# Two bias rows of a fused transformer block: VectorE sums bias times weights, TensorE multiplies once by ones

## The chip, the cores and the metric

One core of one Trainium2 chip runs the whole kernel. The metric is device time in microseconds (us) of one execution; the median of three runs stands for the kernel.

## The reference, cut to what matters

The block is two half-steps of a quantised feed-forward network around one attention, on x of 2 x 2048 rows of 256.

```python
x = x + 0.5 * ffn(layernorm(x))        # network 1
x = x + attn(layernorm(x))             # complex-valued projections, one softmax
x = x + 0.5 * ffn(layernorm(x))        # network 2

# inside attn; Wq, Wk, Wv are [512, 256], Wo is [256, 512], bq, bk, bv are [512]
scores = (qr @ kr.T + qi @ ki.T) / 16
out    = softmax(scores) @ [vr, vi] @ Wo.T + bo
```

ffn quantises its input, its weights and its hidden values in blocks of 16 to a four-bit grid. Attention is computed with products of the weights: M = Wq' Wk and N = Wv' Wo'. Two rows of 256 numbers come from the biases, the key row `bk @ Wq` (name `rk_row`) and the value row `bv @ Wo.T` (name `bias_row`, to which bo is added later). Each has to stand on all 128 partitions. This change is about how these two rows are made.

## The kernel before

The rows of x lie in SBUF as 32 tiles of 128 x 256. Every engine runs a program of its own in order; semaphores (`then_inc`, `wait_ge`) tie them together, and nothing reorders an engine's queue.

**Network 1** is a pipeline of rounds, `step(c, par)` with c from -2 to 29, and a tail for the last two tiles. A round works on several tiles at once. In round c TensorE runs, in this order: the first third of gate and up for tile c+3 (`gate_up`, L1881, its first matmul waits until VectorE has read the same PSUM banks for tile c+2), the transposes of the quantised values of tile c (L1762), the other two thirds of gate and up, and the down projection of tile c (L1892 with the upper halves, L1899 with the rest). Up to round 3 it also makes a product with a negative identity (L1920) for the lower halves; from c = 4 on VectorE makes these instead (`by_vector`, L894 and L896).

VectorE runs in round c: `scales(c + 2)` (L811 block maxima, L814, L824), `to_grid(c + 1)` (L833, L839), `lower(c)` (L894, L896) and `product(c + 3)` (L798, gate times up into `z`). The next thing is L811 of round c+1, which reads that `z` and a normalised tile from ScalarE.

GpSimd (POOL) runs in round c: `negative_scales` (L561, waits for L824), `residual` (L554), `scaled_by_pool(c + 2)` (L569, `y`; `product(c + 3)` waits for it, because it overwrites `z`) and `quantised(c + 1)` (L587, `zq`: three pieces of 256, 704 and 64 columns). If c divides by four it also runs `group_std` (L482 to L490), and if c - 1 does, `output_std` (L497 to L503). L798, L833, L839 and L894 have one operand in PSUM and one in SBUF; L569 and L587 read two tensors in SBUF.

**The bias rows.** Wq lies in SBUF as `wq_s` [128, 4, 256] and Wo transposed as `woT` [128, 4, 256]: 512 rows in four groups of 128. `b3` holds the three biases as [128, 3, 4]. During the start GpSimd spreads bk and bv over 128 columns each (`broadcast_biases`, `bkB` and `bvB`, L540 and L541). Late in network 1, in round 29, TensorE makes the key row (`key_bias_row`): four matmuls of plain float32, one per group, summed in PSUM, with the spread bias as stationary operand, so that every partition receives the row. At the beginning of attention, between the transposes of the second group of keys and the first values, it makes the value row the same way (`value_bias_row`). All of these show as L1769, the line of the helper `product`, and a float32 matmul stands in the trace as two records. ScalarE copies both rows out (`bias_rows`, L1313 and L1314), which frees the bank, and VectorE and GpSimd use them.

At the beginning of attention VectorE runs the lower halves of the keys (L975), `row_term` per tile (L777, needs `rk_row`) and the lower halves of the values (L989); `values(0, 2)` on TensorE waits for the first L989.

Of the kernel before, what the change touches and what calls it, by code (L numbers as in the profile page):

```python
# [9 lines left out]
ALU = mybir.AluOpType  # L10
# [3 lines left out]
P = 128  # L14
# [16 lines left out]
def macaron_kernel(nc, x_in, wq, bq, wk, bk, wv, bv, wo, bo, w_gate, w_up, w_down, out):  # L31
    T, D = x_in.shape
# [7 lines left out]
    KE = E // P  # L40
# [26 lines left out]
    with ctx:  # L67
        def sb(name, shape, dt=F32, at=ctx):
            return at.enter_context(nc.sbuf_tensor(name, shape, dt))
# [4 lines left out]
        def sem(name):  # L74
            return ctx.enter_context(nc.semaphore(name))
# [10 lines left out]
        m_hi = sb("m_hi", [P, KD, D], F32R)  # L86
        m_lo = sb("m_lo", [P, KD, D], F32R)
        nv = sb("nv", [P, KD, 2 * D], F32R)
# [19 lines left out]
        ffn = ExitStack()  # L108
# [14 lines left out]
        wq_s = sb("wq_s", [P, KE, D], at=ffn)  # L123
        woT = sb("woT", [P, KE, D], at=ffn)
        b3 = sb("b3", [P, 3, KE], at=ffn)
        bkB = sb("bkB", [P, KE, P], at=ffn)
        bvB = sb("bvB", [P, KE, P], at=ffn)
        bo_row = sb("bo_row", [P, D], at=ffn)
        mv = sb("mv", [P, NT, 2], at=ffn)
        stats = sb("stats", [P, NT, 6], at=ffn)  # L130
# [55 lines left out]
        rk_sum, bv_sum = bank4[:, 2, 0:D], bank4[:, 2, D:2 * D]  # L186
# [8 lines left out]
        qk_in, wv_in, wo_in, b_in = sem("qk_in"), sem("wv_in"), sem("wo_in"), sem("b_in")  # L195
# [1 line left out]
        x_in_s = [sem(f"x_in{n}") for n in range(len(x_parts))]  # L197
        wc = {k: sem("w_" + k) for k in ("amax", "up", "neg", "inv", "y", "y_pool", "abs", "rnd", "grid", "q", "T", "hi",
                                         "sub", "lo")}
        aw = {k: sem("aw_" + k) for k in ("bcast", "bk", "row", "row_s", "woT", "woT_s", "m", "m_hi", "m_sub", "m_lo", "nv", "nv_hi",  # L200
                                          "nv_sub", "nv_lo", "bq", "bq_s", "rows", "rows_s", "bias")}
        x_tot, x_nm, x_var, x_eps = sem("x_tot"), sem("x_nm"), sem("x_var"), sem("x_eps")
        stat_set, mv_done, g_stats, g_rstd, g_nmr = (sem("stat_set"), sem("mv_done"), sem("g_stats"),
# [41 lines left out]
        def hidden(k):  # L245

            return between(k, 0, NT - 1)

        def ahead(k):

            return between(k, -LEAD, NT - LEAD - 1)
# [5 lines left out]
        def number(f, k):  # L257

            return NCH * f + k + LEAD + 1
# [10 lines left out]
        def whole(f, k):  # L270

            return (3 if f else 2) <= k <= NT - LEAD - 1
# [6 lines left out]
        def wait_scaled(engine, f, k):  # L279

            if hidden(k) and not whole(f, k):
                engine.wait_ge(y_done, scaled_apart(f, k))
            if ahead(k):
                engine.wait_ge(yx_done, NT * f + k + LEAD + 1)
# [27 lines left out]
        def T_bank(k):  # L312

            return bank5[:, 0:2, :] if k == NT - 2 else bank2[:]
# [139 lines left out]
        def _(pool):  # L454
# [80 lines left out]
                pool.wait_ge(aw["m"], 1)  # L535
                nc.gpsimd.tensor_copy(wk_s[:, :, D], b3[:, 1, :]).then_inc(aw["bk"], 1)

            def broadcast_biases():

                nc.gpsimd.tensor_copy(bkB[:], b3[:, 1, :].unsqueeze(2).to_broadcast([P, KE, P]))  # L540
                nc.gpsimd.tensor_copy(bvB[:],  # L541
                                      b3[:, 2, :].unsqueeze(2).to_broadcast([P, KE, P])).then_inc(aw["bcast"], 1)

            def output_bias():

# [72 lines left out]
            weight_q(3)  # L618
            bias_column()
            first_ffn(-5, 1)  # L620
            broadcast_biases()
            first_ffn(-4, 0)
            pool.wait_ge(wc["y"], 2)
            weight_y(5)
# [88 lines left out]
        def _(dve):  # L713
# [6 lines left out]
            def group_statistics(g):  # L720

                tiles = range(4 * g, 4 * g + 4)
                q = slice(tiles[0], tiles[-1] + 1)
                dve.wait_ge(stat_set, tiles[-1] - 7)
                for t in tiles:
                    nc.vector.bn_aggr(mv[:, t, :], stats[:, t, :]).then_inc(mv_done, 1)
                dve.wait_ge(mv_done, tiles[-1] - 7)
                nc.vector.tensor_scalar(out=nmean[:, q], in0=mv[:, q, 0], scalar1=-1.0, scalar2=None,
                                        op0=ALU.mult).then_inc(g_stats, 1)
                nc.vector.tensor_scalar(out=var[:, q], in0=mv[:, q, 1], scalar1=EPS, scalar2=None,  # L730
                                        op0=ALU.add).then_inc(g_stats, 1)
# [59 lines left out]
            def ffn_step(f):  # L791
                def product(t):

                    dve.wait_ge(silu_done, NT * f + t + 1)
                    dve.wait_ge(gu_done, NT * f + t + 1)
                    if t and whole(f, t - 1):
                        wait_scaled(dve, f, t - 1)
                    nc.vector.tensor_tensor(out=z[:, 0:I], in0=gu[:, I:G], in1=silu[:],  # L798
                                            op=ALU.mult).then_inc(gu_read, 1)
# [57 lines left out]
                def blocks_of(c, par):  # L857
                    if c == NT - 3:
                        scales(NT - 1, par)
                        scaled(NT - 1)  # L860
                        to_grid(NT - 2)
                        quantised_late(NT - 2, 1 - par)
                        return
                    if c < -3 and chain(c + 1):
                        to_grid(c + 1)
                    if chain(c + 2):
                        scales(c + 2, par)
                    if f == 0 and c == -2:
                        scaled(c + 2)
                        to_grid(c + 1)  # L870
                        return
                    if c >= -3 and chain(c + 1):
                        to_grid(c + 1)
                    if chain(c + 2) and not whole(f, c + 2):
                        scaled(c + 2)
                    if by_vector(f, c):
                        lower(c, par)

                def input_statistics(c):

                    if c == -2:
                        tile_statistics(8)
                        tile_statistics(9)
                    if c == -1:
                        tile_statistics(10)
                        tile_statistics(11)
                        group_statistics(2)

                def lower(k, par):

                    bank = T_bank(k).rearrange("p a (n t) -> p (a n) t", t=P)
                    dve.wait_ge(hi_done, number(f, k))
                    n = slice(0, HK + KD if ahead(k) else HK)
                    nc.vector.tensor_tensor(out=T_lo[:, par, n, :], in0=bank[:, n, :],  # L894
                                            in1=T_hi[:, par, n, :].bitcast(F32), op=ALU.subtract)
                    nc.vector.tensor_tensor(out=T_hi[HR:P, par, HK + KD, :], in0=bank[HR:P, HK + KD, :],  # L896
                                            in1=T_hi[HR:P, par, HK + KD, :].bitcast(F32),
                                            op=ALU.subtract).then_inc(vector_lo, 1)
# [15 lines left out]
                def quantised_late(k, par):  # L914

                    dve.wait_ge(grid_done, number(f, k))
                    dve.wait_ge(T_done, number(f, k - 1))
                    nc.vector.tensor_tensor(out=blocks(zq[:, 0:I]), in0=blocks(grid[:, 0:I]),
                                            in1=spread(s_neg[:, par, 0:HB], HB), op=ALU.mult)
                    nc.vector.tensor_tensor(out=blocks(zq[:, I:I + HR]), in0=blocks(grid[:, I - HR:I]),  # L920
                                            in1=spread(s_neg[:, par, HB - HR // BLOCK:HB], HR // BLOCK),
                                            op=ALU.mult).then_inc(zq_done, 1)
# [7 lines left out]
                def step(c, par):  # L930
                    blocks_of(c, par)
                    if hidden(c + 3):
                        product(c + 3)
                    if f == 0 and c < 0:
                        input_statistics(c)
                    if c == NT - 2:
                        quantised_late(NT - 1, 1 - par)
                        lower_late(c, par)
                    if c == NT - 1:
                        lower_late(c, par)  # L940
                        if f:
                            residual_last()
# [231 lines left out]
            n = NQ - 1  # L1174
# [581 lines left out]
        def _(pe):  # L1756
# [10 lines left out]
            def product(dst, left, right, first=True):  # L1767
                for j in range(KE):
                    last = nc.tensor.matmul(dst, lhsT=left[:, j, :], rhs=right[:, j, :],  # L1769
                                            start=first and j == 0, stop=j == KE - 1, skip_group_check=True)  # L1770
                return last
# [60 lines left out]

            def key_bias_row():

                pe.wait_ge(aw["bcast"], 1)
                product(rk_sum, bkB, wq_s).then_inc(aw["rows"], 1)

            def value_bias_row():

                product(bv_sum, bvB, woT, False).then_inc(aw["rows"], 1)  # L1840

            def weight_lower(n):

# [415 lines left out]
            n = NQ - 1  # L2259
# [67 lines left out]
```

## Time and profile before

| | |
|---|---|
| median of 3 runs | 908.06 us (907.93 to 908.46) |
| the profiled execution | 908.92 us |
| its span | 907.1 us |
| granted TensorE clock, mean | 1.000 of full speed |
| network 1 in the rows | from about 20 us to 258 us |
| TensorE busy | 884.5 us (98%) |
| VectorE busy | 693.5 us (76%) |
| GpSimd busy | 548.2 us (60%) |

The span is that of the recorded instructions. A busy share is an average over stages: in network 1, network 2 and attention the engines are loaded differently. Matmul records overlap their neighbours, so the time that a matmul takes from its engine is the distance between starts.

### The profile page before, as it was taken

The page shows a single profiled execution, that of the slowest core. Times are in us where ns is not written, and L with a number is a line of the kernel's source. Part 1 is how long each engine was busy: PE and PEld are TensorE (multiplying, and loading weights), DVE is VectorE, ACT ScalarE, POOL GpSimd, SP SyncE. Part 2 cuts the span into 40 slices and gives each one's busy share as a digit, 9 for nine tenths or more (in the row PEclk, how much of TensorE's full clock was granted, in tenths as well). Part 3 has the DMA queues.
Part 4 walks back from the last instruction along what each step waited for, and adds up shares of the span by engine and source line. Part 5 has one row for each costly group of instructions (what it writes and reads, how often), then busy time and mean ns, then how long its engine had stood idle before and what let it go on. Part 6 is the DMA issues. An engine that isn't in the chain of part 4 may idle for free.

```text
span 907.1 us, 16197 instructions
## 1 busy us (share of the span) xinstructions
PE 884.5 (98%) x5608; PEld 796.5 (88%) x5608; DVE 693.5 (76%) x1088; ACT 620.5 (68%) x1383; POOL 548.2 (60%) x618
## 2 busy tenths in 40 slices
PE   4999999999999999999999999999999999999997
PEld 3789999999987898999998899998998899999997
DVE  6987999999976667654564644545599999999998
ACT  6789888877674665768675576767784567555453
POOL 5477889898410264535763154546477778877762
DMA  9200000000000000000000000000000000000001
GB/s 314 66 1 1 1 1 2 1 1 1 1 1 1 1 1 1 1 1 2 1 1 1 1 1 1 1 1 1 1 1 1 1 24 24 25 24 24 1 24 47
DMA packets 11952, 13.81 MB, mean 15 GB/s; under 512 B 864, under 2 KB 11104, under 8 KB 11872
## 3 DMA queue, kind: packets, MB, share of 16 engines
q1 hardware_dynamic: 11872, 12.79, 4.2%
q8 instruction: 45, 0.74, 0.3%
q14 instruction: 35, 0.29, 0.1%
HBM read 8.59 MB, written 4.19 MB: 14 GB/s over the span
## 4 chain that ended last, share of the span: by engine, by line
PE 88%; DVE 5%; ACT 2%; issue 2%; POOL 2%; DMA 1%; SPq 0%; DVEq 0%; POOLq 0%; ACTq 0%
PE bank L1881 24%; PE bank L2135 19%; PE bank_b L1892 7%; PE bank L1762 7%; PE bank_b L1899 5%; PE bank L2175 4%; PE bank L2177 4%; PE bank L2173 4%; PE bank L2098 2%; PE bank_b L2177 1%; PE bank_b L2173 1%; PE bank_b L2175 1%; PE bank L2116 1%; PE bank_b L2116 1%; DMA wk_s<-in_L_attn_Wk 1%
## 5 line engine op out<-in xcount | busy, mean ns | idle before, releaser
L637 POOL TENSOR_TENSOR p_lo<-s_ring,p_hi 128x512 fp32r<-128x512 f32 x128 | 167.3, 1311 | 217.6 <-ACT p_hi L1620 217.6
L1004 DVE TENSOR_TENSOR top<-bank,top 128x512 f32<-128x512 f32 x112 | 77.4, 691 | 125.7 <-ACT s_ring L1604 125.6
L587 POOL TENSOR_TENSOR zq<-grid,s_neg 128x256 f32<-128x256 f32 (+2 forms) x184 | 141.9, 798 | 14.3 <-DVE grid L839 14.3
L1881 PE MATMUL bank<-w_hi,T_hi 128*128 128x512 f32 (+1 forms) x384 | 148.8, 387 | 1.3 <-DVE z L798 0.9
L1881 PE MATMUL bank<-w_hi,T_lo 128*128 128x512 f32 (+1 forms) x384 | 144.0, 375 | 0.0
L1881 PE MATMUL bank<-w_lo,T_hi 128*128 128x512 f32 (+1 forms) x384 | 143.6, 374 | 0.0
L1604 ACT ACTIVATE s_ring<-bank 128x512 f32<-128x512 f32 x128 | 75.9, 593 | 78.0 <-PE bank L2135 77.9
L1425 ACT ACTIVATE T_hi<-bank 128x1024 fp32r<-128x1024 f32 (+1 forms) x68 | 64.7, 951 | 84.9 <-PE bank L1762 84.9
L2173 PE MATMUL bank<-v_hl,p_hi 128*128 128x258 f32 x384 | 110.0, 286 | 0.4 <-DVE x L1036 0.2
L2175 PE MATMUL bank<-v_hl,p_hi 128*128 128x256 f32 x384 | 108.3, 282 | 0.0
L2177 PE MATMUL bank<-v_hl,p_lo 128*128 128x258 f32 x384 | 108.3, 282 | 0.0
L569 POOL TENSOR_TENSOR y<-z,s_inv 128x960 f32<-128x960 f32 (+1 forms) x56 | 98.5, 1758 | 8.9 <-DVE s_inv L824 4.5
L2135 PE MATMUL bank<-q_hi,k_hi 128*128 128x512 f32 x256 | 101.3, 396 | 0.8
L2135 PE MATMUL bank<-q_lo,k_hi 128*128 128x512 f32 x256 | 100.7, 393 | 0.0
L2135 PE MATMUL bank<-q_hi,k_lo 128*128 128x512 f32 x256 | 100.3, 392 | 0.0
L1610 ACT ACTIVATE s_ring<-s_ring 128x512 f32<-128x512 f32 x128 | 79.2, 622 | 18.5 <-DVE s_ring L1026 18.5
L1026 DVE TENSOR_TENSOR s_ring<-s_ring,bank 128x512 f32<-128x512 f32 x128 | 84.9, 678 | 1.3 <-PE bank L1762 0.9
L1620 ACT ACTIVATE p_hi<-s_ring 128x512 fp32r<-128x512 f32 x128 | 80.7, 631 | 7.1 <-PE bank_b L2177 3.5
L811 DVE TENSOR_REDUCE amax<-z 128x60 f32<-128x960 f32 (+2 forms) x72 | 74.9, 1041 | 11.8 <-ACT z L1459 9.0
L1881 PEld LDWEIGHTS bank<-w_hi,T_hi 128*128 128x128 f32 x384 | 72.3, 188 | 11.3 <-issue 1.2
L1881 PEld LDWEIGHTS bank<-w_hi,T_lo 128*128 128x128 f32 x384 | 72.2, 188 | 10.6
L1892 PE MATMUL bank_b<-wd_hl,T_hi 128*128 128x256 f32 x600 | 80.4, 280 | 0.1
(239 smaller groups left out, 2232.0 us busy)
## 6 DMA issues: line engine op xcount, KB each, us to landing
out<-x SPq DMA_DIRECT2D x7, 512.0 KB, 2.9
x<-in_L_attn_hidden_states SPq DMA_DIRECT2D x3, 1024.0 KB, 12.2
x<-in_L_attn_hidden_states SPq DMA_DIRECT2D x2, 512.0 KB, 7.7
wraw<-in_L_ffn_w_down SPq DMA_DIRECT2D x1, 704.0 KB, 7.5
wraw<-in_L_ffn_w_up SPq DMA_DIRECT2D x1, 640.0 KB, 5.5
wq_s<-in_L_attn_Wq SPq DMA_DIRECT2D x1, 512.0 KB, 7.1
wk_s<-in_L_attn_Wk SPq DMA_DIRECT2D x1, 512.0 KB, 8.0
wo_s<-in_L_attn_Wo SPq DMA_DIRECT2D x1, 512.0 KB, 8.3
```

The source lines that it names most:

```text
L569: nc.gpsimd.tensor_tensor(out=blocks(y[:, lo:Z]), in0=blocks(z[:, lo:Z]), in1=spread(s_inv[:, lo // BLOCK:ZB], (Z - lo) // BLOCK), op=ALU. ...
L587: last = nc.gpsimd.tensor_tensor(out=blocks(zq[:, to:to + hi - lo]), in0=blocks(grid[:, lo:hi]), in1=spread(s_neg[:, par, lo // BLOCK:hi / ...
L637: nc.gpsimd.tensor_tensor(out=lower_buf(n, c), in0=score_buf(n, c), in1=upper_buf(n, c).bitcast(F32), op=ALU.subtract).then_inc(plo_done, 1)
L1026: nc.vector.tensor_tensor(out=p, in0=p, in1=shift_bank, op=ALU.subtract).then_inc(diff_done, 1)
L1610: nc.scalar.activation(p, p, ACT.Exp, scale=SCALE).then_inc(exp_done, 1)
L1620: nc.scalar.activation(upper_buf(n, c), score_buf(n, c), ACT.Copy).then_inc(phi_done, 1)
L1881: last = nc.tensor.matmul(gu[:, lo:hi], lhsT=T[:, par, HK + kd, :], rhs=w[:, kd, lo:hi], start=n == 0, stop=n == len(terms) - 1)
L1892: nc.tensor.matmul(dn, lhsT=T_hi[:, par, k, :], rhs=wd_hl[:, k, half:half + D], start=n == 0, stop=False)
L2135: last = nc.tensor.matmul(score_bank(c), lhsT=kk[:, kd, t], rhs=q[:, kd, :], start=i == 0, stop=i == len(terms) - 1)
L2173: nc.tensor.matmul(o[:, 0:D + 2], lhsT=hi[:, q], rhs=v_hl[:, c, 0:D + 2], start=c == 0, stop=False, skip_group_check=True)
L2175: nc.tensor.matmul(o[:, 0:D], lhsT=hi[:, q], rhs=v_hl[:, c, D + 2:], start=False, stop=False, skip_group_check=True)
L2177: last = nc.tensor.matmul(o[:, 0:D + 2], lhsT=lo[:, q], rhs=v_hl[:, c, 0:D + 2], start=False, stop=c == CH - 1, skip_group_check=True)
```

## The change

VectorE now sums bias times weights over the four groups ahead of time, in eight instructions: for each row one `tensor_scalar` and three `scalar_tensor_tensor` over 128 x 256 float32, all operands in SBUF. They stand in VectorE's queue behind `product(c + 3)` of rounds 4, 6, 8, ..., 18 of network 1. What is left is a sum over partitions, which TensorE makes with one float32 matmul per row and a square of ones as stationary operand. GpSimd writes that square with one memset, where it spread the biases with two copies. SBUF space of the two spread biases goes to `bias_sum` and `ones_sq`. `product(dst, left, right)` is the loop of four matmuls.

```diff
-            def broadcast_biases():
-                nc.gpsimd.tensor_copy(bkB[:], b3[:, 1, :].unsqueeze(2).to_broadcast([P, KE, P]))
-                nc.gpsimd.tensor_copy(bvB[:],
-                                      b3[:, 2, :].unsqueeze(2).to_broadcast([P, KE, P])).then_inc(aw["bcast"], 1)
+            def all_ones():
+                nc.gpsimd.memset(ones_sq[:], 1.0).then_inc(aw["ones"], 1)
...
             first_ffn(-5, 1)
-            broadcast_biases()
+            all_ones()
             first_ffn(-4, 0)
...
+                def bias_part(i):
+                    n, j = i // KE, i % KE
+                    weights = (wq_s, woT)[n]
+                    if i == 0:
+                        dve.wait_ge(b_in, 16 * 4)
+                        dve.wait_ge(qk_in, 16 * 2)
+                    if i == KE:
+                        dve.wait_ge(aw["woT_s"], 2)
+                    if j == 0:
+                        nc.vector.tensor_scalar(out=bias_sum[:, n, :], in0=weights[:, 0, :], scalar1=b3[:, 1 + n, 0:1],
+                                                scalar2=None, op0=ALU.mult).then_inc(aw["sum"], 1)
+                    else:
+                        dve.wait_ge(aw["sum"], i)
+                        nc.vector.scalar_tensor_tensor(out=bias_sum[:, n, :], in0=weights[:, j, :],
+                                                       scalar=b3[:, 1 + n, j:j + 1], in1=bias_sum[:, n, :],
+                                                       op0=ALU.mult, op1=ALU.add).then_inc(aw["sum"], 1)
...
                     if hidden(c + 3):
                         product(c + 3)
+                    if f == 0 and 4 <= c < 4 + 4 * KE and c % 2 == 0:
+                        bias_part(c // 2 - 2)
...
             def key_bias_row():
-                pe.wait_ge(aw["bcast"], 1)
-                product(rk_sum, bkB, wq_s).then_inc(aw["rows"], 1)
+                pe.wait_ge(aw["ones"], 1)
+                pe.wait_ge(aw["sum"], KE)
+                nc.tensor.matmul(rk_sum, lhsT=ones_sq[:], rhs=bias_sum[:, 0, :], start=True, stop=True,
+                                 skip_group_check=True).then_inc(aw["rows"], 1)
             def value_bias_row():
-                product(bv_sum, bvB, woT, False).then_inc(aw["rows"], 1)
+                pe.wait_ge(aw["sum"], 2 * KE)
+                nc.tensor.matmul(bv_sum, lhsT=ones_sq[:], rhs=bias_sum[:, 1, :], start=False, stop=True,
+                                 skip_group_check=True).then_inc(aw["rows"], 1)
```

## Rows read from the trace of the kernel before

**Rows 1.** The page: VectorE's busy tenths in 40 slices of the span.

```profile
DVE  6987999999976667654564644545599999999998
```

**Rows 2.** Window of four rounds: us, busy PE, PEld, DVE, ACT, POOL, clock.

```profile
137.30:164.02 26.72, 26.72 (x175) 24.50 (x174) 25.10 (x33) 23.31 (x72) 23.28 (x31) 1.00 0.01 1
```

**Rows 3.** VectorE's timeline in network 1: start, us, line, [idle before].

```profile
84.45 0.89 DVE L798 TENSOR_TENSOR z<-bank,silu 128x704 f32<-128x704 f32 x1
85.43 1.15 DVE L811 TENSOR_REDUCE amax<-z 128x60 f32<-128x960 f32 x1
...
97.83 0.89 DVE L798 TENSOR_TENSOR z<-bank,silu 128x704 f32<-128x704 f32 x1 [0.18 <-POOL y L569]
...
104.32 0.89 DVE L798 TENSOR_TENSOR z<-bank,silu 128x704 f32<-128x704 f32 x1
...
184.06 0.89 DVE L798 TENSOR_TENSOR z<-bank,silu 128x704 f32<-128x704 f32 x1
185.21 1.15 DVE L811 TENSOR_REDUCE amax<-z 128x60 f32<-128x960 f32 x1 [0.25 <-ACT z L1459]
```

**Rows 4.** TensorE's timeline: first matmul of a round.

```profile
85.49 0.47 PE L1881 MATMUL bank<-w_hi,T_hi 128*128 128x512 f32 x1
...
185.79 0.40 PE L1881 MATMUL bank<-w_hi,T_hi 128*128 128x512 f32 x1
```

**Rows 5.** GpSimd's timeline; x2 are the 256 and the 704 piece.

```profile
83.98 1.97 POOL L587 TENSOR_TENSOR zq<-grid,s_neg 128x256 f32<-128x256 f32 x2
...
97.66 1.97 POOL L587 TENSOR_TENSOR zq<-grid,s_neg 128x256 f32<-128x256 f32 x2
```

**Rows 6.** Durations (ns, min/median/max) of VectorE instructions of 128 x 256, all in SBUF.

```profile
L777 DVE SCALAR_TENSOR_TENSOR st_junk<-x,nmean,rk_row x32: 474/480/1612, 264.5 to 395.1; 128x256 f32<-128x256 f32 x32
L1075 DVE TENSOR_SCALAR xn<-x,nmean,rstd x6: 397/404/1414, 454.1 to 459.1; 128x256 f32<-128x256 f32 x6
```

**Rows 7.** Timeline: VectorE and GpSimd at the same time.

```profile
309.48 1.60 DVE L777 SCALAR_TENSOR_TENSOR st_junk<-x,nmean,rk_row 128x256 f32<-128x256 f32 x1
309.51 1.29 POOL L637 TENSOR_TENSOR p_lo<-s_ring,p_hi 128x512 fp32r<-128x512 f32 x1 [0.37 <-ACT p_hi L1620]
...
458.74 1.74 DVE L1075 TENSOR_SCALAR xn<-x,nmean,rstd 128x256 f32<-128x256 f32 x2
459.03 1.30 POOL L637 TENSOR_TENSOR p_lo<-s_ring,p_hi 128x512 fp32r<-128x512 f32 x1 [1.38 <-ACT p_hi L1620]
```

**Rows 8.** TensorE's timeline at the two bias rows and at `values(0, 2)`.

```profile
246.35 1.89 PE L1769 MATMUL bank<-wq_s,bkB 128*128 128x256 f32 x8
247.89 0.82 PE L1920 MATMUL bank<-T_hi,neg_ident 128*128 128x512 f32 x2
...
261.78 1.89 PE L1769 MATMUL bank<-woT,bvB 128*128 128x256 f32 x8
263.32 0.59 PE L2116 MATMUL bank<-nv,k_hi 128*128 128x256 f32 x2
...
267.11 0.48 PE L2116 MATMUL bank<-nv,k_hi 128*128 128x256 f32 x2
```

**Rows 9.** Timelines of ScalarE and VectorE beside the bias rows.

```profile
246.57 1.01 ACT L1425 ACTIVATE T_hi<-bank 128x1024 fp32r<-128x1024 f32 x1
...
253.53 0.22 DVE L920 TENSOR_TENSOR zq<-grid,s_neg 128x64 f32<-128x64 f32 x1
...
263.03 1.23 DVE L975 TENSOR_TENSOR k_lo<-bank,k_hi 128x1024 fp32r<-128x1024 f32 x1 [0.46 <-ACT k_hi L1369]
...
265.92 0.69 DVE L989 TENSOR_TENSOR v_hl<-bank,v_hl 128x512 fp32r<-128x512 f32 x1
```

**Rows 10.** Timeline of the start: VectorE and GpSimd.

```profile
24.30 0.61 POOL L540 COPY bkB<-b 128x512 f32<-128x512 f32 x1
24.32 0.63 DVE L819 SCALAR_TENSOR_TENSOR s_neg<-amax,c_neg 128x16 f32<-128x16 f32 x1
...
48.17 0.89 DVE L798 TENSOR_TENSOR z<-bank,silu 128x704 f32<-128x704 f32 x1
```

More of the change, by code:

```diff
@@ L125, in macaron_kernel @@
         b3 = sb("b3", [P, 3, KE], at=ffn)
-        bkB = sb("bkB", [P, KE, P], at=ffn)
-        bvB = sb("bvB", [P, KE, P], at=ffn)
+        bias_sum = sb("bias_sum", [P, 2, D], at=ffn)
+        ones_sq = sb("ones_sq", [P, P], at=ffn)
         bo_row = sb("bo_row", [P, D], at=ffn)
@@ L199, in macaron_kernel @@
                                          "sub", "lo")}
-        aw = {k: sem("aw_" + k) for k in ("bcast", "bk", "row", "row_s", "woT", "woT_s", "m", "m_hi", "m_sub", "m_lo", "nv", "nv_hi",
+        aw = {k: sem("aw_" + k) for k in ("ones", "sum", "bk", "row", "row_s", "woT", "woT_s", "m", "m_hi", "m_sub", "m_lo", "nv", "nv_hi",
                                           "nv_sub", "nv_lo", "bq", "bq_s", "rows", "rows_s", "bias")}
```

## The prediction, made before the changed kernel was run

> **What bounds the kernel now.** I read the page first, its totals (in the table above) and then its slices: TensorE is busy nearly always, VectorE three quarters of the span, but VectorE's slices stand at 9 through most of network 1, where its eight new instructions go [rows 1]. So the question is whether VectorE has room there. Then comes a window of four rounds: from 137.30 on they take 26.72 us, TensorE is busy in all of it, VectorE for 25.10 [rows 2]. VectorE's own timeline shows the room more sharply. The shortest distance between two L798 is 6.49 us (97.83 to 104.32), against 26.72 / 4 = 6.68 for TensorE, and in a settled round VectorE waits 0.25 us for ScalarE ahead of L811 [rows 3]. That is 0.19 to 0.25 us of room per round.
>
> How late VectorE may be is seen from L798's end to TensorE's first matmul of the next round. In the first round that matters it is 85.49 - (84.45 + 0.89) = 0.15 us, which is as tight as it gets: TensorE waits there. Late in the stage it is 185.79 - (184.06 + 0.89) = 0.84 [rows 3, 4]. So VectorE starts with no reserve at round 4 and has saved up 0.84 - 0.15 = 0.69 us by round 19.
>
> **The change part by part.** *The eight VectorE instructions.* The nearest rows for their size: a `scalar_tensor_tensor` of 128 x 256 with all operands in SBUF takes 0.48 us in the median but 1.61 at most, a `tensor_scalar` 0.40 and 1.41 [rows 6]. The long ones are explained by GpSimd. At 309.48 the vector instruction meets a GpSimd one that ends at 309.51 + 1.29 = 310.80; it ends at 311.08, 0.28 later. At 458.74 the second of two `tensor_scalar` meets one that ends at 460.33 and ends itself at 460.48, 0.15 later [rows 7]. So such an instruction runs only when GpSimd's instruction is through, and then takes 0.28 or 0.15 us. The Trainium skill says the same ("SBUF — State Buffer", section "SBUF: two separate sides"): the port pair that the two engines share is an exclusive lock for a whole instruction, and it bears on vector instructions with two SBUF inputs or in a two-port mode. By that rule the sum is the one worked out next; it speaks against this change, since VectorE's big instructions in these rounds each have an operand in PSUM and the new ones don't.
>
> What does GpSimd do when the new instruction comes up, directly behind L798? In round 4 its 256 and 704 pieces of `zq` begin at 83.98 and end at 85.95, which is 1.50 us behind L798's start at 84.45. In round 6 they end at 99.63, 1.80 behind the start at 97.83 [rows 3, 5]. L798 is through 0.9 us behind its start. So all eight come up inside the 704 piece. This isn't chance: the distance hangs on GpSimd's chain behind L824 of the same round, so it moves with VectorE when VectorE gets late. The next L811 then starts about 1.75 us behind L798's start (0.65 + 0.98 with `tensor_scalar`) in place of 0.98 (84.45 to 85.43): 0.75 us, or 0.65. In the rounds like 6, where GpSimd is late from its two extra groups (L798 waits 0.18 for it there [rows 3]), it is 2.05 - 0.98, about 1.05.
>
> Now VectorE over four rounds. From L798 of round 4 to that of round 6: 2 x 6.49 + 0.65 = 13.63. GpSimd alone gives 97.83 - 84.45 = 13.38, and 0.25 for being held by the new instruction in its turn, also 13.63. From round 6 to 8: 2 x 6.49 + 1.05 = 14.03. Sum 27.66, against TensorE's 26.72: 0.94 too much. Three such groups bring L798 of round 16 to 84.45 + 83.0 = 167.4, and that of round 19 comes 13.63 + 1.05 + 6.49 = 21.2 later, at 188.6. Before it stood at 184.06 [rows 3]. VectorE is 4.5 us late, less the reserve of 0.69: TensorE stalls 3.8 us, spread over rounds 5 to 19, a part in nearly every second one. After the last of them VectorE's room hides the rest, and the stall stays in the span, since TensorE has no idle time to take it from.
>
> *The key row.* Its four matmuls take 247.89 - 246.35 = 1.54 us [rows 8]; three of four are 1.16. But they stand ahead of L1920, which waits for ScalarE's `T_hi`, and that ends at 246.57 + 1.01 = 247.58 [rows 9]. So L1920 can come at 247.7 at best, 0.2 us earlier. Behind it VectorE works without a pause on the last two tiles and ends its `zq` at 253.75 [rows 9], which the last transposes wait for; it gains next to nothing from this. I take 0.1 us (bounds 0 and 0.25).
>
> *The value row.* Again 263.32 - 261.78 = 1.54, so 1.16 less [rows 8]. Values follow at once and need nothing from it. What is late next is the first lower half of values on VectorE, which stands behind L975 (263.03 to 264.26 [rows 9], unmoved, since it waits for ScalarE's keys) and two `row_term` of some 0.5 us [rows 6], and takes 0.69 itself [rows 9]: it ends at about 264.26 + 1.1 + 0.7 = 266.1. The values that wait for it start at 267.11 now and would want to come at 267.11 - 1.16 = 265.95 [rows 8]. So I take 1.0 us (bounds 0.8 and 1.16).
>
> *GpSimd's start.* Two copies go, the first of 0.61 us [rows 10], and one memset comes. Meanwhile VectorE's L819 of 16 columns takes 0.63 us, most of it held by the copy [rows 10]. About 0.5 us come free on VectorE. But its queue is fed again by the first L798, which waits for TensorE, and TensorE's round waits for the third L798 (48.17 [rows 10]), up to which VectorE has no pause. I take 0.05 us (bounds 0 and 0.35, the idle time of ScalarE and TensorE on that way). The added waits cost nothing: GpSimd used the same biases at 24.30 [rows 10], 60 us before the first of the eight, and the last one comes up near 182, over 60 us before TensorE asks for the key row at 246.35 [rows 8].
>
> Sum: + 3.8 - 0.1 - 1.0 - 0.05 = + 2.65 us. The profiled execution took 908.92 us for a span of 907.1, 0.9 above the median of 908.06; against the median the forecast is **910.7 us**. Some 1.8 us (0.2%) is what a measurement of this kernel can tell from no change.
>
> **The rivals.**
> *A, the forecast:* held, 910.7, own range 909.5 to 911.8. A milder form has the two engines share the way instead of locking it: each costs some 0.4 + 0.27, a pair 1.34, four rounds 25.96 + 1.34 = 27.3, which over 15 rounds and with 0.3 for the first is a stall of 2.5 and 909.4. 65% in all.
> *B, not slower:* the eight aren't held. Place: VectorE between L798 and L811; price 0.4 us each (0.48 less the overlap), 25.96 + 0.8 = 26.76 in four rounds, just TensorE's pace. The stall is 0.4 (0.2 of it at round 5, where there is no reserve), 1.15 come off: 907.3. It decides as soon as an instruction costs under some 0.5 us, where the stall falls under 1.15. For it: the median rows are short. Against it: the phase of the 704 piece. 18%.
> *C, faster:* as B, and both bias rows give their whole 1.16: 2.3 less 0.3, 906.0. Against it: `T_hi` ends 0.3 us ahead of L1920 [rows 8, 9]. 5%.
> *D, worse:* the new instruction gets its turn only behind the 64 piece too, and GpSimd's `zq` gets late for the transposes: 0.3 us more in each of eight, 913.1. For it: the three pieces follow each other without a gap. Against it: nothing in the rows shows a vector instruction passed over. 12%.
>
> **How the numbers follow.** The time is A's. The range reaches down to B with its scatter and up to D: 906.9 to 913.1; C and the tails are left out. Slower by over 0.2%: A without its milder part, 55%, and D, 12%: 67%. Within: the rest of A, 10%, and B: 28%. Faster: C, 5%.
>
> **What would show it.** The eight instructions of 128 x 256 should take 0.6 to 1.2 us in the trace and end 0.15 or 0.28 us behind a 704 piece; if they take 0.4 to 0.5, B holds. Four rounds between L798 of rounds 4 and 20 should take 27.6 us, not 26.7, with TensorE idle ahead of L1881 and released by L798. L1920 of round 29 should come right behind `T_hi`, with TensorE idle for about 1 us ahead of it. The first values' lower half should set `values(0, 2)`. The prediction is wrong if GpSimd's pieces move away from L798 once VectorE is late, or if VectorE catches up between two new instructions by more than 0.2 us per round.

## The result, and the profile after

The changed kernel takes 910.84 us (median of 8 runs, 910.55 to 911.29), the kernel before 908.09 (median of 8, 907.76 to 908.55). The ratio is 1.003, its 95% interval 1.002 to 1.0039: slower by some 2.7 us, against a forecast of 910.7. The profiled execution has a span of 909.5 us (before 907.1) at a granted clock of 1.00 of full speed (mean).

The totals and VectorE's slices on the page of the changed kernel:

```profile
PE 885.0 (97%) x5596; PEld 793.9 (87%) x5596; DVE 697.8 (77%) x1096; ACT 621.4 (68%) x1383; POOL 549.1 (60%) x617
DVE  7987999999986766665573644545599999999998
```

VectorE's slices hardly differ from [rows 1] (the last one of network 1 is at 8 for 7): tenths are too coarse for this change. The line numbers have moved: L796 is the L798 of the rows before, L809 the L811, L585 the L587, L1903 the L1881, L1921 the L1899 and L1942 the L1920. The windows view, four rounds at a time, from one L796 to the fourth behind it (columns as in rows 2):

```profile
84.06:111.67 27.61, 27.37 (x171) 24.48 (x171) 26.79 (x35) 22.39 (x67) 23.52 (x31) 1.00 0.00 1
111.67:139.41 27.74, 27.48 (x174) 24.74 (x173) 26.91 (x34) 22.68 (x69) 23.65 (x31) 1.00 0.00 1
139.41:167.03 27.62, 27.35 (x174) 24.70 (x173) 26.78 (x34) 23.46 (x71) 23.53 (x31) 1.00 0.01 2
```

Four rounds take 27.6 to 27.7 us (forecast 27.66), where they took 26.72 at TensorE's own pace [rows 2]. (The first two groups of four, from round 4 and from round 8, took 26.37 and 26.48 between two L798 before, because VectorE was catching up there.) VectorE is busy for 26.8 of them, 1.7 more than the 25.1 before, and what is left is 0.8 us, the few hundredths between its instructions. TensorE, which had no idle time there, has some in every one. The group that costs it, from the view of one tile (ns: min/median/max, then first and last start):

```profile
L901 DVE SCALAR_TENSOR_TENSOR bias_sum<-wq_s,b,bias_sum x3: 973/1272/1277, 98.5 to 126.2; 128x256 f32<-128x256 f32 x3
L901 DVE SCALAR_TENSOR_TENSOR bias_sum<-woT,b,bias_sum x3: 973/1273/1276, 153.9 to 181.6; 128x256 f32<-128x256 f32 x3
...
L897 DVE TENSOR_SCALAR bias_sum<-wq_s,b x1: 847/847/847, 84.9 to 84.9; 128x256 f32<-128x256 f32 x1
L897 DVE TENSOR_SCALAR bias_sum<-woT,b x1: 846/846/846, 140.2 to 140.2; 128x256 f32<-128x256 f32 x1
```

Why they take that long is seen in the timeline of round 6, first VectorE, then GpSimd:

```profile
97.68 0.89 DVE L796 TENSOR_TENSOR z<-bank,silu 128x704 f32<-128x704 f32 x1
98.48 1.28 DVE L901 SCALAR_TENSOR_TENSOR bias_sum<-wq_s,b,bias_sum 128x256 f32<-128x256 f32 x1
99.69 1.14 DVE L809 TENSOR_REDUCE amax<-z 128x60 f32<-128x960 f32 x1
...
105.18 0.89 DVE L796 TENSOR_TENSOR z<-bank,silu 128x704 f32<-128x704 f32 x1
```

```profile
95.72 1.82 POOL L567 TENSOR_TENSOR y<-z,s_inv 128x960 f32<-128x960 f32 x1
97.51 2.40 POOL L585 TENSOR_TENSOR zq<-grid,s_neg 128x256 f32<-128x256 f32 x3
101.73 0.41 POOL L559 TENSOR_SCALAR s_neg<-amax 128x60 f32<-128x60 f32 x1 [1.81 <-DVE s_inv L822]
```

The 256 and 704 pieces of `zq` take 1.97 us together [rows 5], so the second ends at 97.51 + 1.97 = 99.48. The new instruction starts at 98.48 and ends at 99.76, 0.28 behind that. Then L809 starts at 99.69, 2.01 behind L796, where it stood 0.98 behind it before [rows 3]. GpSimd's third piece, 64 columns, pays too: the three take 2.40 us here and 2.23 in the round before, which has no new instruction. The last row shows what GpSimd does with the delay: it waits 1.81 us for VectorE's scales. Both engines are late, and GpSimd has no more work than before. Of VectorE's 1.28 us only 0.48 are work: that is what the same kind of instruction takes alone [rows 6].

The waits view for 85 to 200 us (in total, times, longest):

```profile
POOL s_neg L559 <- DVE s_inv L822: 13.5, 12, 1.8
PEld bank_b L1921 <- DVE T_hi L912: 2.0, 5, 0.5
...
PE bank_b L1921 <- DVE T_hi L912: 1.0, 4, 0.3
```

And TensorE's timeline at one of the waits:

```profile
105.20 0.50 PE L1921 MATMUL bank_b<-wd_hl,T_hi 128*128 128x256 f32 x2 [0.24 <-DVE T_hi L912]
105.55 0.75 PE L1921 MATMUL bank_b<-wd_hl,T_lo 128*128 128x256 f32 x5
106.22 0.47 PE L1903 MATMUL bank<-w_hi,T_hi 128*128 128x512 f32 x1
```

L1903 starts 0.15 us behind the end of L796 (105.18 + 0.89 = 106.07), the distance at which TensorE waited in the first tight round before. The idle time that the profile names, though, stands one step earlier, ahead of L1921, which wants the last lower part of `T` that VectorE makes just ahead of L796.

The two bias rows on TensorE, and the values that are late next:

```profile
249.96 0.60 PE L1855 MATMUL bank<-bias_sum,ones_sq 128*128 128x256 f32 x2
251.25 0.73 PE L1942 MATMUL bank<-T_hi,neg_ident 128*128 128x512 f32 x2 [0.69 <-ACT T_hi L1443]
...
265.12 0.60 PE L1861 MATMUL bank<-bias_sum,ones_sq 128*128 128x256 f32 x2
265.36 0.58 PE L2138 MATMUL bank<-nv,k_hi 128*128 128x256 f32 x2
```

The account, in the differences of start against the same instruction before: at L796 of round 4 the kernel is 0.39 us early (84.06 for 84.45), at that of round 19 it is 4.22 late (188.28 for 184.06). The reserve takes up part of that, and at L796 of round 28, the last tile, it is 3.61 late (247.57 for 243.96): TensorE has lost 4.0 us. The first matmul of the queries is 3.34 late, so the key row gave 0.27. The first matmul of the scores is 2.28 late, so the value row gave 1.06. From there to the end of the span it is 638.5 us before and 638.6 after.

### The profile page after: what moved, and what is told of

Read it like the earlier page. It is cut to its first block, busy times and chain, and to the rows that moved or that the text cites. A ratio compares the mean times of both kernels' runs of the same rounds, so it can differ in the third digit from the quotient of the medians.

```text
span 909.5 us, 16181 instructions
## 1 busy us (share of the span) xinstructions
PE 885.0 (97%) x5596; PEld 793.9 (87%) x5596; DVE 697.8 (77%) x1096; ACT 621.4 (68%) x1383; POOL 549.1 (60%) x617
## 4 chain that ended last, share of the span: by engine, by line
PE 72%; DVE 4%; POOL 3%; issue 1%; ACT 1%; DVEq 0%; POOLq 0%
PE bank L2157 19%; PE bank L1903 16%; PE bank_b L1914 5%; PE bank L1780 5%; PE bank L2199 4%; PE bank L2197 4%; PE bank L2195 4%; PE bank_b L1921 4%; PE bank L2120 2%; POOL p_lo L635 2%; PE bank_b L2199 1%; PE bank_b L2195 1%; PE bank_b L2197 1%; PE bank L2138 1%; PE bank_b L2138 1%
## 5 line engine op out<-in xcount | busy, mean ns | idle before, releaser
L585 POOL TENSOR_TENSOR zq<-grid,s_neg 128x256 f32<-128x256 f32 (+2 forms) x184 | 143.1, 805 | 13.8 <-DVE grid L837 13.8
L1903 PE MATMUL bank<-w_hi,T_hi 128*128 128x512 f32 (+1 forms) x384 | 149.3, 389 | 1.2 <-DVE z L796 1.1
L1903 PE MATMUL bank<-w_hi,T_lo 128*128 128x512 f32 (+1 forms) x384 | 143.8, 374 | 0.0
L1903 PE MATMUL bank<-w_lo,T_hi 128*128 128x512 f32 (+1 forms) x384 | 143.4, 374 | 0.0
L1903 PEld LDWEIGHTS bank<-w_hi,T_hi 128*128 128x128 f32 x384 | 72.2, 188 | 11.8 <-issue 1.2
L809 DVE TENSOR_REDUCE amax<-z 128x60 f32<-128x960 f32 (+2 forms) x72 | 74.8, 1038 | 9.0 <-ACT z L1477 6.1
L1903 PEld LDWEIGHTS bank<-w_hi,T_lo 128*128 128x128 f32 x384 | 72.1, 188 | 10.8
```

Of the source, the lines that this page charges most:

```text
L585: last = nc.gpsimd.tensor_tensor(out=blocks(zq[:, to:to + hi - lo]), in0=blocks(grid[:, lo:hi]), in1=spread(s_neg[:, par, lo // BLOCK:hi / ...
L1903: last = nc.tensor.matmul(gu[:, lo:hi], lhsT=T[:, par, HK + kd, :], rhs=w[:, kd, lo:hi], start=n == 0, stop=n == len(terms) - 1)
```

## The experiments

Experiments 1 to 4 are compared with the kernel before at a median of 908.37 us, experiments 5 to 7 with it at 907.99, each measured alongside. Differences of a few tenths between the two sets are not read. Each diff is against the changed kernel, and waits that belong to a changed line change with it where they are not shown. The question is how much of the 2.7 us is VectorE's held instructions, whether the hold is GpSimd's lock or simply the place of more work, and whether TensorE's gain is real by itself.

**1. VectorE's part alone.**

```
-                nc.gpsimd.memset(ones_sq[:], 1.0).then_inc(aw["ones"], 1)
+                nc.gpsimd.tensor_copy(bkB[:], b3[:, 1, :].unsqueeze(2).to_broadcast([P, KE, P]))
+                nc.gpsimd.tensor_copy(bvB[:],
+                                      b3[:, 2, :].unsqueeze(2).to_broadcast([P, KE, P])).then_inc(aw["bcast"], 1)
...
-                nc.tensor.matmul(rk_sum, lhsT=ones_sq[:], rhs=bias_sum[:, 0, :], start=True, stop=True,
-                                 skip_group_check=True).then_inc(aw["rows"], 1)
+                product(rk_sum, bkB, wq_s).then_inc(aw["rows"], 1)
...
-                nc.tensor.matmul(bv_sum, lhsT=ones_sq[:], rhs=bias_sum[:, 1, :], start=False, stop=True,
-                                 skip_group_check=True).then_inc(aw["rows"], 1)
+                product(bv_sum, bvB, woT, False).then_inc(aw["rows"], 1)
```

> VectorE's eight instructions stay in rounds 4 to 18, their sums are not used; the bias rows are made as before (two copies on GpSimd, four matmuls each). If the stall in network 1 is VectorE's alone, its L798 distances are those of the changed kernel (four rounds 27.6 to 27.7 us) and nothing is given back: about 908.1 + 3.9 = 912.0 us. If part of the stall came from TensorE's or GpSimd's new queue, it is clearly under that, 911 or less.

Measured: 912.23 us (911.62 to 912.46, 5 runs), ratio 1.0042 (1.0028 to 1.0055). The start of L796 goes from 0.84 early in round 4 to 3.23 late in the last one: 4.07 us. The eight instructions are the same ones, 0.84 to 0.85 and 0.98 to 1.28 us. So VectorE's part costs about 4 us by itself, and the new matmuls on TensorE have no share in it.

**2. TensorE's part alone.**

```
+                nc.gpsimd.memset(bias_sum[:], 0.0)
                 nc.gpsimd.memset(ones_sq[:], 1.0).then_inc(aw["ones"], 1)
...
-                    if f == 0 and 4 <= c < 4 + 4 * KE and c % 2 == 0:
-                        bias_part(c // 2 - 2)
```

> The eight VectorE instructions are left out (GpSimd writes zeros into the sums during the start, so the two bias rows are zero); one matmul per row. Theory of the prediction: 0.1 + 1.0 + 0.05 come off, 906.9 us. What the trace of the changed kernel shows (0.4 at the start, 0.25 at the key row, 1.05 at the value row) gives 906.4. Rival: the removed matmuls come off whole, 2.6 us, 905.5.

Measured: 906.68 us (906.35 to 906.95, 11 runs), ratio 0.9981 (0.9972 to 0.999). Every distance between two L796 of network 1 is that of before to some hundredths. The gain stands in the two places: 0.27 us behind the key row and 1.06 behind the value row, 1.3 in the trace for 1.7 (plus or minus 0.8) in the medians. The whole 1.16 for each is out.

**3. The same eight instructions in other slots of the round.** Behind the block maximum, where GpSimd has finished `zq` and waits for the scales, in two neighbouring rounds of each four.

```
+            BIAS_AT = (7, 8, 11, 12, 15, 16, 19, 20)
...
                                             apply_absolute_value=True).then_inc(amax_done, 1)
+                    if f == 0 and k - 2 in BIAS_AT:
+                        bias_part(BIAS_AT.index(k - 2))
...
-                    if f == 0 and 4 <= c < 4 + 4 * KE and c % 2 == 0:
-                        bias_part(c // 2 - 2)
```

> The same eight instructions, with the same operands, but between L809 and L812 of rounds 7, 8, 11, 12, 15, 16, 19, 20, where GpSimd stands idle and waits for VectorE's scales. Theory of the hold: none of them meets a GpSimd instruction, each takes 0.40 to 0.48 us, four rounds take 26.7 to 26.9, and what the matmuls and the start give stays: 906.5 to 907.3 us. Rival, VectorE has no room for this work wherever it stands (0.75 to 1.05 us are what such an instruction costs in these rounds): 910.8 as the changed kernel.

Measured: 908.58 us (908.28 to 909.15, 11 runs), ratio 1.0003 (0.9995 to 1.0012). The instructions ran as expected, but the kernel is 1.3 us slower than the expectation allows. Two rows of its VectorE timeline, at different times:

```profile
99.47 0.35 DVE L811 TENSOR_SCALAR bias_sum<-wq_s,b 128x256 f32<-128x256 f32 x1
...
233.42 0.74 DVE L839 SCALAR_TENSOR_TENSOR s_neg<-amax,c_neg 128x44 f32<-128x44 f32 x1
```

The first is a bias instruction, not held: 0.35 us for the 0.85 of the changed kernel, and the `scalar_tensor_tensor` take 0.48 for 0.97 to 1.28. So the place makes the price, and over half of it is waiting. The second is far behind the last bias instruction and explains part of the miss. It is an old instruction of 44 columns, and GpSimd's row at that time is

```profile
233.31 0.79 POOL L552 TENSOR_TENSOR x<-x,down 128x256 f32<-128x256 f32 x1 [1.25 <-ACT down L1434]
```

The rounds themselves lost 0.77 us (L796's counterpart from 0.44 early to 0.33 late): four rounds take 26.8 to 26.9, just over TensorE's 26.72, and VectorE arrives in the last rounds with less reserve: in round 25 its product ends 0.61 us ahead of TensorE's next first matmul, for 0.84 before. In the rounds that follow, a small VectorE instruction and GpSimd's residual come up almost together, and the one that starts first decides. In the kernel before `s_neg` starts 0.12 us ahead of the residual in round 26 and takes 0.20; here it starts 0.11 behind and takes 0.74. In experiment 1 it is ahead by just 0.02, and is not held; its rows, first VectorE, then GpSimd:

```profile
236.41 0.20 DVE L820 SCALAR_TENSOR_TENSOR s_neg<-amax,c_neg 128x44 f32<-128x44 f32 x1
```

```profile
236.43 0.78 POOL L555 TENSOR_TENSOR x<-x,down 128x256 f32<-128x256 f32 x1 [1.37 <-ACT down L1435]
```

In experiment 3 one small instruction in each of rounds 26, 27 and 28 is held: 0.74, 0.57 and 0.65 us in place of 0.20. The first queries are 1.28 late, 0.95 more than at round 26, although the key row gives back 0.27 ahead of them: 1.2 us for the tail. 0.8 + 1.2 = 2.0, and the run is 1.9 above experiment 2.

**4. The same place, a quarter of the columns.**

```
-                        nc.vector.tensor_scalar(out=bias_sum[:, n, :], in0=weights[:, 0, :], scalar1=b3[:, 1 + n, 0:1],
+                        nc.vector.tensor_scalar(out=bias_sum[:, n, 0:D // 4], in0=weights[:, 0, 0:D // 4], scalar1=b3[:, 1 + n, 0:1],
...
-                        nc.vector.scalar_tensor_tensor(out=bias_sum[:, n, :], in0=weights[:, j, :],
+                        nc.vector.scalar_tensor_tensor(out=bias_sum[:, n, 0:D // 4], in0=weights[:, j, 0:D // 4],
```

> The eight instructions at their place, on 64 of 256 columns (the other three quarters of both sums are left out and zero). Theory of the hold: only the streaming gets shorter (0.2 us of scalar_tensor_tensor, 0.1 of tensor_scalar); they still end right behind the 704 piece and last 0.65 to 1.1 us; four rounds 27.2 to 27.3, 909.2 to 909.6 us. Rival, the cost is the work itself or a shared rate, in proportion to the width: 0.2 us each, hidden, 906.5 to 907 us.

Measured: 909.54 us (909.11 to 910.86, 11 runs), ratio 1.0016 (1.0007 to 1.0024). A quarter of the work still costs two thirds: four rounds take 27.3 us. VectorE and GpSimd in round 6:

```profile
98.11 1.07 DVE L902 SCALAR_TENSOR_TENSOR bias_sum<-wq_s,b,bias_sum 128x64 f32<-128x64 f32 x1
```

```profile
97.13 2.23 POOL L586 TENSOR_TENSOR zq<-grid,s_neg 128x256 f32<-128x256 f32 x3
```

The 704 piece ends at 97.13 + 1.97 = 99.10, the instruction at 99.18, 0.08 behind it where the full one is 0.28 behind. All eight are 0.75 to 1.08 us, 0.1 to 0.2 shorter than the full ones, and three quarters of the columns are gone. That rules out the milder form of A, in which two engines share the way and a shorter instruction is shorter in proportion. From round 4 to round 25 the rounds lose 2.73 us (the changed kernel has lost 4.06 there). The profiled execution then has the held small instructions of experiment 3 as well (0.75, 0.57 and 0.64 us) and is the slowest of the eleven, 910.86; 1.3 us less for that tail is 909.5, the median. That most of the others were spared the tail is inferred from this sum, not seen.

**5. All eight instructions in VectorE's pause behind network 1.** Both rows are then made just ahead of the values.

```
             first_residual_last()
+            for i in range(2 * KE):
+                bias_part(i)
...
                         pe.wait_ge(gu_read, NT)
-                        key_bias_row()
...
             transpose_keys(0, 1)
+            key_bias_row()
             value_bias_row()
```

(The call of `bias_part` in the rounds goes, as in experiment 3.)

> All eight instructions in one row behind VectorE's last residual of network 1, where VectorE waits 2.3 us for ScalarE's queries and GpSimd is idle; both bias rows are made next to each other at the place of the value row. Theory of the hold: 0.35 to 0.42 us each, 2.9 in all, of which 0.6 stand out of the pause and delay only the lower halves of the queries, which TensorE needs 6 us later; network 1 is that of the kernel without them. 906.7 to 907.0 us, as the kernel with one matmul and no vector work (906.7). Rival: VectorE's work is paid for there too, since keys, values and row terms follow: 908 and more.

Measured: 906.77 us (906.63 to 907.58, 11 runs), ratio 0.9987 (0.9979 to 0.9996). VectorE's timeline of the pause:

```profile
257.38 0.41 DVE L943 SCALAR_TENSOR_TENSOR x<-bank,x 128x256 f32<-128x256 f32 x1
257.71 0.34 DVE L799 TENSOR_SCALAR bias_sum<-wq_s,b 128x256 f32<-128x256 f32 x1
258.09 1.52 DVE L803 SCALAR_TENSOR_TENSOR bias_sum<-wq_s,b,bias_sum 128x256 f32<-128x256 f32 x3
259.53 0.35 DVE L799 TENSOR_SCALAR bias_sum<-woT,b 128x256 f32<-128x256 f32 x1
259.91 1.52 DVE L803 SCALAR_TENSOR_TENSOR bias_sum<-woT,b,bias_sum 128x256 f32<-128x256 f32 x3
261.36 1.40 DVE L997 SCALAR_TENSOR_TENSOR q_lo<-bank,bqk,q_hi 128x512 fp32r<-128x512 f32 x2
```

and GpSimd's, which says why nothing holds them:

```profile
256.49 0.74 POOL L552 TENSOR_TENSOR x<-x,down 128x256 f32<-128x256 f32 x1 [2.40 <-ACT down L1432]
263.25 0.74 POOL L545 TENSOR_TENSOR bias_row<-bias_row,bo_row 128x256 f32<-128x256 f32 x1 [6.03 <-ACT bias_row L1332]
```

Eight instructions that cost 4 us in the rounds take 3.7 us of VectorE's time here and cost nothing that is seen. The 3.7 are more than the 2.9 expected, since a `scalar_tensor_tensor` takes 0.48 us here too. L997 follows at once, 1.0 us later than before if the 0.2 by which this trace is early are taken off, and no wait of TensorE comes of it: from the first values to the first scores it is 5.28 us, as before. At the scores this trace has gained 1.14 us where experiment 2 has 1.33; the 0.2 belong to the key row's matmul, which stands ahead of the values now. The median is under that of the kernel before by 1.2 us (0.1%, interval 0.04 to 0.21%), and under that of the changed kernel by about 4.

**6. A mixture:** the key's four in the slots of experiment 3 (rounds 7, 8, 11 and 12), the value's four in the pause.

```
+            BIAS_AT = (7, 8, 11, 12)
...
             first_residual_last()
+            for i in range(KE, 2 * KE):
+                bias_part(i)
```

> The four instructions of the key row between L809 and L812 of rounds 7, 8, 11, 12, the four of the value row in the pause behind the last residual. Theory: the kernel with all eight in such slots lost some 0.7 us in rounds 26 to 28, where a late VectorE ran into GpSimd's residual (L552) with small instructions; with only four, VectorE has caught up before that, so four rounds take 26.7 to 26.8 and the last L796 distances are 6.98, 6.45, 6.39 as before: 906.8 to 907.3 us. Rival: the losses at the end have nothing to do with how late VectorE is: 907.5 to 908.

Measured: 906.95 us (906.64 to 907.65, 11 runs), ratio 0.9986 (0.9977 to 0.9995). The run is there for experiment 3's miss: VectorE has time to catch up behind round 12. The start of `z` (L816 here) goes from 0.76 early in round 4 to 0.15 late in round 14 and back to 0.46 early in round 20, and stays there, 0.3 us lost in all. In the last rounds the small instruction now passes ahead of GpSimd's residual, first VectorE, then GpSimd:

```profile
232.63 0.20 DVE L839 SCALAR_TENSOR_TENSOR s_neg<-amax,c_neg 128x44 f32<-128x44 f32 x1
```

```profile
232.75 0.74 POOL L552 TENSOR_TENSOR x<-x,down 128x256 f32<-128x256 f32 x1 [1.47 <-ACT down L1436]
```

The distances of the last three rounds are 6.97, 6.45 and 6.39 us, those of before, against 6.98, 6.98 and 6.55 in experiment 3. VectorE's product of round 26 ends 0.54 us ahead of TensorE's next first matmul, as before, against 0.31 in experiment 3. So the 1.2 us of that tail hang on some 0.2 us of VectorE's reserve, as the trace of experiment 3 suggested.

**7. Experiment 2 with GpSimd's two copies kept.**

```
+                nc.gpsimd.tensor_copy(bkB[:], b3[:, 1, :].unsqueeze(2).to_broadcast([P, KE, P]))
+                nc.gpsimd.tensor_copy(bvB[:], b3[:, 2, :].unsqueeze(2).to_broadcast([P, KE, P]))
+                nc.gpsimd.memset(bias_sum[:], 0.0)
                 nc.gpsimd.memset(ones_sq[:], 1.0).then_inc(aw["ones"], 1)
```

> As the kernel with one matmul per row and no vector work (sums left out, both rows zero), but GpSimd still makes the two copies during the start, ahead of its memsets. Theory of the prediction: what the copies cost VectorE is covered, at most 0.1 us more than without them, 906.7 to 906.8. Rival, taken from the start of the changed kernel's trace, which is 0.4 us ahead: 907.0 to 907.1.

Measured: 906.77 us (906.37 to 907.93, 11 runs), ratio 0.9988 (0.9979 to 0.9997), against 0.9981 (0.9972 to 0.999) without the copies. The intervals overlap: the copies are worth some tenths at most. The traces say the same. The second `z` starts 0.3 to 0.9 us earlier than in the trace of before in all eight new traces, and the two that keep the copies are 0.84 and 0.93 early.

## Why the prediction was right, step by step

**The hold.** It was the main term, and it held in form and size. All eight instructions start 0.80 to 0.81 us behind L796, inside the 704 piece, and end 0.28 to 0.29 (`scalar_tensor_tensor`) or 0.16 (`tensor_scalar`) behind its end. Experiments 3, 4 and 5 show the mechanism from three sides: away from GpSimd's pieces the same instruction takes 0.48 us and not 1.27; with a quarter of the columns in the old place it still takes 1.07; in the pause the eight are free. That the place directly behind L796 is slow for another reason doesn't fit either: in rounds 8 and 16 the `scalar_tensor_tensor` comes up 1.28 us behind the start of `zq` and takes 0.97 us, in rounds 6, 10, 14 and 18 it comes up 0.97 to 0.99 behind and takes 1.27 to 1.28. No run moved GpSimd's pieces themselves. The rule cited in the prediction from the Trainium skill ("SBUF — State Buffer", section "SBUF: two separate sides") agrees with all of that. The same section says that a GpSimd instruction that only writes SBUF doesn't contend with a VectorE instruction of two SBUF inputs, and one pair of rows agrees: in experiment 4, GpSimd's memset of 512 columns at 23.88 (0.52 us) and VectorE's two-input instruction of 16 columns at 23.89 (0.16 us) ran side by side:

```profile
23.89 0.16 DVE L818 SCALAR_TENSOR_TENSOR s_neg<-amax,c_neg 128x16 f32<-128x16 f32 x1
```

```profile
23.88 0.52 POOL L540 MEMSET bias_sum<- 128x512 f32 x1
```

Before, the same instruction took 0.63 us beside GpSimd's copy, which reads SBUF [rows 10].

**VectorE's lateness.** Forecast 27.66 per four rounds, measured 27.61, 27.74 and 27.62; forecast 4.5 by round 19, measured 0.39 + 4.22 = 4.6. **TensorE's stall:** forecast 3.8, measured 4.0, and 4.07 in experiment 1. The term was too small by 0.2: VectorE was late by 4.6 and not 4.5, and from round 19 to 28 it won back 0.6 and not 0.69. Where it shows was told only in part: L1903 does start 0.15 behind L796's end, but the named idle time stands ahead of L1921, released by the end of `T`'s lower part on VectorE. Also, the profile shows TensorE idle for only 0.24 to 0.27 us in windows that are 0.9 to 1.0 longer than the 26.72 of TensorE's own pace. The rest stands in records that got longer, such as first matmuls of 0.50 us where 0.40 is usual, and in the waits of weight loads, so distances between the same instruction are the safer measure of a stall.

**The key row.** Forecast 0.1, bound 0.25, measured 0.27 to 0.28, just outside the bound, in the changed kernel and in experiments 2, 6 and 7. It is 0.27 in experiment 5 too, where no key row stands in that place at all, so it isn't the matmuls that limit it. The limit was told rightly: L1942 waits 0.69 for ScalarE's `T_hi` at 251.20. What was mis-sized is what lies behind: the last tile's work on ScalarE and VectorE moved up with it (the L831 of the last `zq` is 3.40 late where L796 is 3.61), and I had taken VectorE as the bound there, working "without a pause". It does wait there: before, that last L833 starts at 250.87, when ScalarE's `silu` has ended at 250.78. The idle time forecast as about 1 us is 0.69.

**The value row.** The saving ahead of the values was forecast as 1.16, three quarters of 1.54. Measured is 1.30: the first values start 0.24 behind the one matmul (265.12 to 265.36), so a row of four had 1.54 and one has 0.24. Then 0.24 is given back: L1007 ends at 268.55 + 0.69 = 269.24 and `values(0, 2)` starts at 269.39, 2.28 late, the first lower half of values being what sets it, as forecast. Net 1.06, forecast 1.0.

The size of this term is right, but the prediction reached it by a step that it didn't check. It gave VectorE 1.1 us for the two `row_term` ahead of that lower half, from the median of [rows 6]. In the kernel before they took 1.66 us at this very place (264.26 to 265.92), because the first one waited for ScalarE's copy of the value row and was then held by GpSimd's addition of bo, which starts on the same copy. First VectorE, then GpSimd, before:

```profile
264.47 0.99 DVE L777 SCALAR_TENSOR_TENSOR st_junk<-x,nmean,rk_row 128x256 f32<-128x256 f32 x1 [0.21 <-ACT bias_row L1314]
```

```profile
264.44 0.74 POOL L547 TENSOR_TENSOR bias_row<-bias_row,bo_row 128x256 f32<-128x256 f32 x1 [6.73 <-ACT bias_row L1314]
```

and in the changed kernel:

```profile
267.52 0.58 DVE L775 SCALAR_TENSOR_TENSOR st_junk<-x,nmean,rk_row 128x256 f32<-128x256 f32 x1
```

```profile
267.08 0.73 POOL L545 TENSOR_TENSOR bias_row<-bias_row,bo_row 128x256 f32<-128x256 f32 x1 [6.03 <-ACT bias_row L1332]
```

The shorter value row brings copy and addition forward, the wait is gone and all but a tenth of the hold, and the two take 0.96 us (267.59 to 268.55). Experiments 2 and 7 show the same (0.59 and 0.58 for the first one), and experiment 1, with four matmuls, has the 0.99 back. Had the 1.66 stayed, `values(0, 2)` would have started 0.7 us later, and the value row would have given some 0.4 (an estimate from these rows). That the forecast of 1.0 came true rests on an effect that it doesn't name, and to that extent it is luck.

**The start.** Forecast 0.05. The first L796 waited 0.60 us for TensorE, so what VectorE gained ahead of it ends there, as said. All eight new traces are early at the second `z`, the two that keep the copies too (experiments 1 and 7), so this isn't the edit's doing. It fits the trace of before instead, whose execution took 908.92 us, 0.9 above the median; the changed kernel's took 911.29, 0.45 above its own. The difference, 0.4, is about the 0.39 by which the trace is early at round 4. The other traces fit, experiment 4 with its tail apart: the later the second `z`, the longer the profiled execution against the median of its own kernel (0.93 early and at the median in experiment 2, 0.29 early and 0.8 above it in experiment 5). So executions of one kernel differ ahead of the second `z`. What varies there was not looked for.

**The sum:** +4.0 - 0.27 - 1.06 = +2.7 at the scores without the start, and the medians differ by 2.7; with the start it is +2.3, and the spans differ by 2.4. The forecast time is within 0.2 us of the measured one, closer than its terms deserve: the stall was 0.2 larger than forecast, and the two savings together 0.2 larger, which cancels. Experiments 1 and 2, which are the two halves, give +3.9 and -1.7 in the medians, together +2.2, which differs from 2.7 by less than their intervals (over 1 us and 0.8 us to either side).

**The rivals.** B (not held) fails on the durations: 0.85 to 1.28 us and not 0.4 to 0.5. C fails on experiment 2, which holds all of TensorE's gain and stops at 1.7. A's milder form fails on experiment 4, and on the full instructions, which take 0.85 to 1.28 us and not some 0.67. D fails on the end times: the instruction gets its turn between the 704 and the 64 piece, and the 64 piece is 0.17 late for it. B's world does exist, though, in experiment 5: with the hold gone the change saves 1.2 us.

## What to carry to other kernels

Before moving work to an engine that looks a quarter free, look at the timeline of the exact slot: room per round was 0.25 us here, and one added instruction cost 0.6 to 1.0 us of the round for 0.35 to 0.48 us of work, because GpSimd was in the middle of a long instruction. Work that isn't needed until later belongs in a pause that both engines have (experiment 5: no cost seen, and 4 us in the rounds), even if the instruction count is the same. And an engine that has spent a part of its reserve meets collisions it used to clear: experiment 3 lost more behind its last added instruction (1.2 us) than up to it (0.8).

## What the runs showed of the hardware

A held instruction ends at the end of GpSimd's instruction plus a part that goes with its own columns: 0.28 us for 256 and 0.08 for 64 (`scalar_tensor_tensor`), 0.16 and 0.05 (`tensor_scalar`, which has only one tensor in SBUF and was held all the same). It is let in between two GpSimd instructions that follow each other without a gap. The three pieces of `zq` then take 2.40 to 2.42 us for 2.23 at 256 columns (2.27 with `tensor_scalar`), and still 2.23 at 64.

A hold is not a matter of size: `s_neg` of 128 x 44, a 0.20 us instruction, took 0.74 beside GpSimd's 0.79 us residual of 128 x 256. Three such holds stand in the rounds where experiment 3 lost the 0.7 us by which its last `z` fell further behind. In these rows the instruction that starts first has its way, even where it is ahead by only 0.02 us (experiment 1).

Of four float32 matmuls of 128 x 256 in a row, three left out saved 1.30 us of 1.54. The one that stays takes 0.24 us until the next starts, though its records read 0.38 us each.
